# Weights loaded beside their low parts, one explicit order of calls per engine, and a causal mask added in float32r instead of bfloat16

## The chip, the cores and the metric

The kernel runs on one core of a Trainium2 chip. A core has a matrix engine (TensorE, in the profile PE, with its weight loads apart as PEld), a vector engine (VectorE, DVE), an activation engine (ScalarE, ACT), a general engine (GpSimd, POOL) and a queue engine (SyncE, SP) that issues transfers. Each engine works through its own list of instructions in order, and waits on semaphores for the others. The metric is the device time of one execution in microseconds (us), lower is better.

## What is computed

One pre-norm decoder layer on x of 8 batch elements x 256 tokens x 256 features, all in float32:

```python
x = x + attn(layernorm(x))        # 16 heads of 16, rotary positions, causal mask, softmax
x = x + xattn(layernorm(x), ctx)  # 16 heads of 64, 77 context rows, a mask of (8, 256, 77)
x = x + ffn(layernorm(x))         # 256 -> 1024 -> 256, gelu, weights fake-quantised to 8 bits, plus LoRA
...
def fake_quant_weight(w, bits=BITS):
    qmax = 2.0 ** (bits - 1) - 1
    scale = jnp.max(jnp.abs(w)) / qmax
    wq = jnp.clip(jnp.round(w / scale), -qmax - 1, qmax) * scale
```

## The kernel before, in words

**Precision.** Most products are made of three float32r products: a tensor is split into a high part (a copy to float32r by ACT, `split_hi` for weights) and a low part (the tensor less its high part, by DVE, `split_lo` for weights), and `product` on PE adds high x high, high x low and low x high.

**Elements and steps.** The 8 batch elements pass through a pipeline. `step(a, b, n, m)` works at once on the causal attention of element a, on the cross attention and feed-forward part (FFN) of element b = a - 1, on the projections and rotary turn of n = a + 1, and on the first normalisation of m = a + 2. `first()` fills the pipeline, then come `step(0, None, 1, 2)`, `step(1, 0, 2, 3)`, a hardware loop of four equal steps, two steps in which less and less is left to prefetch, and `step(None, 7, None, None)`, which has only the cross attention and FFN of the last element. What stands ahead of `step(1, 0, 2, 3)` is called the start here. Each engine has its own `first` and `step`, and the order of calls in these is the order of its instructions: nothing else schedules.

**The start.** Besides element 0's attention it prepares nine weights. `load_raw` brings a weight into one of two staging halves of `work`; from the third weight on the queue waits for the weight before the last to be split (`w_lo`). Seven of the nine are loaded by POOL's queue, from where POOL also stores the keys and values of the context (`store_keys`, `store_values`) into a scratch tensor in memory. `keys` and `values2` compute these for all elements at once. The two FFN weights are quantised: `largest` (DVE, a row maximum), `quantiser` (POOL, a maximum over partitions), `scale`, three `quantise` parts and `add_lora` (DVE), the LoRA product itself by `lora_up` and `lora_down` on PE.

**Causal attention of one element.** PE's `scores` adds per pair of heads a mask of -2^100 above the diagonal, by a product of an identity with a table, and then the products of queries and keys; DVE's `maxima` takes each row's largest value, `split_max` and `transpose_max` turn it, SP writes it into `q_stack` beside the queries. Then `shifted` (PE) makes the transposed scores less the maximum, `exponentials` (ACT) their exp, `causal` (POOL) zeroes what lies above the diagonal, `weigh` (PE) multiplies by the values, `unnormalised` (ACT) copies, `turn_a` (PE), `attention` (DVE), `turn_back_a`, `output_a` (PE) and `residual_a` (DVE) follow, then `statistics_b` and `norm_b`.

**Cross attention of one element**, in four groups g of heads: `scores2` (PE), `softmax2` (DVE), `exponentials2` (ACT), `sums2` (DVE), `normalise` (POOL), `transpose2` (PE), `probabilities2` (ACT), `weigh2` (PE), `context_hi` (ACT), `context_lo` (DVE), `output2` (PE). The waits that bind most:

```python
pe.wait_ge(c2_lo, 4 * b + g)                      # transpose2(b, g): the group before is split
pe.wait_ge(s_max, H * a + 2 * g - 1)              # scores(a, g): a ring of three banks
dve.wait_ge(rot_ok, 2 * a + w)                    # rotary(a, 1): POOL has read the first half
```

## Time and profile before

| | us |
|---|---|
| median of 3 runs | 733.86 (733.33 to 735.71) |
| the profiled execution | 731.91 |
| its span, first to last instruction | 730.3 |
| PE busy in the span | 580.2 |
| DVE busy | 368.7 |
| ACT busy | 276.5 |
| POOL busy | 189.8 |

The rows further down come from the profiled execution. A row of the timeline gives the start in us from the span's start, the length, the engine, the line of the program, the instruction and its operands (out<-in), and in brackets how long the engine stood idle ahead of it and what ended that. A row by form gives a group's busy time and the mean length in ns. A row of the windows gives each engine's busy time in a stretch and PEclk, the granted TensorE clock as a share of 2.4 GHz.

### The profile page before, as it was taken

Reading aid. Unit: us, or ns where it says so; the run is one execution under the profiler, and the core shown is the slowest. Engines: PE = TensorE matmul, PEld = TensorE weight load, DVE = VectorE, ACT = ScalarE, POOL = GpSimd, SP = SyncE. Lnnn points to the kernel's source line nnn. Section 1 sums busy time; section 2 is a strip of 40 time slices with the busy share of each in tenths; the row PEclk is TensorE's granted clock in tenths of the full one; section 3 lists DMA queues with packets and bytes.
Section 4 is the critical chain, followed back from the end, with each engine's and each line's share of the span. In section 5 each row is a group of like instructions: output and inputs, shape, how many; then the busy total and the mean of one; then the engine's idle time right before and its main releaser. Section 6 shows DMA issues by size and latency. Waiting matters only on the chain.

```text
span 730.3 us, 12418 instructions
## 1 busy us (share of the span) xinstructions
PE 580.2 (79%) x4740; PEld 477.1 (65%) x4740; DVE 368.7 (50%) x711; ACT 276.5 (38%) x419; POOL 189.8 (26%) x295
## 2 busy tenths in 40 slices
PE   3578746498799888987898789878996899688756
PEld 3475323476587657865796579656975687568546
DVE  4455434675347633674357435743575247525521
ACT  2242241233454245333633463336343533363313
POOL 4433223041404122312232223223321301130210
PEclk9789655799799959997999989988998799999968
DMA  6756736020413041203211331123012310200000
GB/s 208 180 185 254 240 116 104 0 87 2 106 37 101 1 99 45 99 1 73 68 67 34 68 73 57 44 55 86 34 54 47 96 31 1 48 9 15 1 0 15
DMA packets 53077, 51.86 MB, mean 71 GB/s; under 512 B 22753, under 2 KB 48769, under 8 KB 53041
## 3 DMA queue, kind: packets, MB, share of 16 engines
q1 hardware_dynamic: 49120, 35.40, 18.9%
q0 software_dynamic: 3920, 15.97, 6.2%
q8 instruction: 24, 0.39, 0.2%
q14 instruction: 13, 0.10, 0.0%
HBM read 33.04 MB, written 18.06 MB: 70 GB/s over the span
## 4 chain that ended last, share of the span: by engine, by line
PE 60%; DVE 16%; issue 8%; ACT 7%; POOL 3%; DMA 1%; POOLq 0%; DVEq 0%; ACTq 0%
PE banks L518 13%; PE banks L519 11%; PE banks L520 11%; PE banks L649 4%; PE banks L744 3%; PE banks L755 3%; DVE mneg L1249 3%; PE banks L662 3%; PE banks L628 3%; DVE c_lo L1208 2%; ACT probs L993 2%; PE banks L622 2%; POOL probs L456 2%; DVE sm L1326 2%; PE banks L699 1%
## 5 line engine op out<-in xcount | busy, mean ns | idle before, releaser
L1249 DVE TENSOR_REDUCE mneg<-banks 128x3 f32<-128x384 f32 x128 | 66.3, 546 | 34.1 <-PE banks L628 34.1
L445 POOL TENSOR_TENSOR work<-work,rc 128x616 f32<-128x616 f32 x32 | 38.9, 1217 | 163.5 <-DVE rc L1328 163.5
L993 ACT ACTIVATE probs<-banks 128x768 f32<-128x768 f32 x64 | 50.1, 811 | 79.1 <-PE banks L649 78.2
L456 POOL TENSOR_SCALAR_AFFINE_SELECT probs<-probs 128x256 f32<-128x256 f32 x128 | 51.2, 430 | 99.5 <-ACT probs L993 99.5
L1208 DVE TENSOR_TENSOR q_lo<-work,q_hi 128x512 fp32r<-128x512 f32 x32 | 22.1, 689 | 73.5 <-ACT q_hi L957 73.5
L518 PE MATMUL banks<-k_hi,q_hi 128*128 128x256 f32 (+1 forms) x160 | 52.7, 329 | 4.3 <-DVE wpj_lo L1182 2.2
L744 PE MATMUL banks<-ident,work 128*77 128x128 f32 x256 | 35.4, 282 | 25.8 <-DVE c_lo L1208 19.7
L957 ACT ACTIVATE work<-banks 77x1024 f32<-77x1024 f32 x32 | 32.4, 1013 | 53.3 <-PE banks L744 53.3
L518 PE MATMUL banks<-wo_hi,c_hi 128*128 128x256 f32 x128 | 42.0, 328 | 12.3 <-DVE c_lo L1208 12.3
L649 PE MATMUL banks<-q_stack,k_stack 50*128 50x128 f32 (+1 forms) x256 | 40.3, 428 | 9.9 <-ACT probs L993 9.9
L744 PEld LDWEIGHTS banks<-ident,work 128*77 128x77 f32 x256 | 28.3, 149 | 29.7 <-POOL work L445 16.2
L519 PE MATMUL banks<-k_lo,q_hi 128*128 128x256 f32 (+1 forms) x160 | 47.1, 294 | 0.0
L520 PE MATMUL banks<-k_hi,q_lo 128*128 128x256 f32 (+1 forms) x160 | 47.0, 294 | 0.0
L649 PEld LDWEIGHTS banks<-q_stack,k_stack 50*128 50x128 f32 x256 | 27.3, 276 | 25.4 <-ACT probs L993 17.8
L1021 ACT ACTIVATE work<-work 128x616 f32<-128x616 f32 x32 | 22.9, 716 | 55.0 <-DVE work L1320 55.0
L518 PE MATMUL banks<-xbT_hi,wfc_hi 128*128 128x256 f32 x128 | 42.4, 331 | 1.5 <-ACT xbT_hi L957 1.5
L662 PE MATMUL banks<-probs,v_aug 128*32 128x256 f32 x256 | 27.1, 505 | 20.7 <-POOL probs L456 20.7
L1208 DVE TENSOR_TENSOR c_lo<-banks,c_hi 128x512 fp32r<-128x512 f32 x32 | 22.0, 688 | 38.6 <-ACT c_hi L957 38.6
L518 PE MATMUL banks<-xbT_hi,wq_hi 128*128 128x256 f32 x128 | 36.7, 287 | 5.0 <-ACT xbT_hi L957 2.9
L519 PE MATMUL banks<-wo_lo,c_hi 128*128 128x256 f32 x128 | 39.6, 309 | 0.0
L520 PE MATMUL banks<-wo_hi,c_lo 128*128 128x256 f32 x128 | 39.6, 309 | 0.0
L519 PE MATMUL banks<-xbT_lo,wfc_hi 128*128 128x256 f32 x128 | 39.0, 305 | 0.0
(184 smaller groups left out, 1684.1 us busy)
## 6 DMA issues: line engine op xcount, KB each, us to landing
rot_dram<-rot_s_hi SPq DMA_DIRECT2D x16, 256.0 KB, 2.1
rot_dram<-rot_s_lo SPq DMA_DIRECT2D x16, 256.0 KB, 2.1
q_stack<-rot_dram SPq DMA_DIRECT2D x32, 128.0 KB, 2.7
k_stack<-rot_dram SPq DMA_DIRECT2D x32, 128.0 KB, 3.2
k_hi<-k_dram SPq DMA_DIRECT2D x16, 154.0 KB, 3.3
k_lo<-k_dram SPq DMA_DIRECT2D x16, 154.0 KB, 3.6
v<-v_dram SPq DMA_DIRECT2D x8, 308.0 KB
x_in<-in_x SPq DMA_DIRECT2D x8, 256.0 KB, 3.0
```

What stands on the lines that cost most here:

```text
L445: pool.tensor_tensor(sc2[g % 2], sc2[g % 2], rc2[:, g % 2].rearrange("p g a -> p g a ()").broadcast_to([P, 4, 2, S2]), ALU.mult).then_inc( ...
L456: last = pool.affine_select(out=diagonal, in_=diagonal, compare_op=ALU.is_ge, fill=0.0, base=0, pattern=[[0, 2], [1, P]], channel_multipli ...
L518: pe.matmul(dst, w[0], x_[0], start=first, stop=False, **kw)
L519: pe.matmul(dst, w[0], x_[1], start=False, stop=False, **kw)
L520: return pe.matmul(dst, w[1], x_[0], start=False, stop=last, **kw)
L649: mm = pe.matmul(halves(bk + p)[:, 1 - k, k * P:T], k_stack[rows, g, k * P:(k + 1) * P], q_stack[rows, g, k * P:T], start=(k == 1), stop=( ...
L662: pe.matmul(dst[32 * j:32 * j + 32, :], v_aug[:, 0, 4 * g + j, :], probs[:, (4 * g + j) % 8, P:3 * P], start=True, stop=False, skip_group_ ...
L744: mm = pe.transpose(bank[0:S2, 5 + c, p * T + q * P:p * T + (q + 1) * P], sc2[g % 2][:, c * QT + q, p, :], ident[:])
L957: act.activation(dst, src, ACT.Copy).then_inc(done, 1)
L993: act.activation(probs[:, n:n + 2, :], bank[:, bk:bk + 2, P:4 * P], ACT.Exp, scale=SCALE).then_inc(p_ok, 1)
L1208: dve.tensor_tensor(dst, src, hi.bitcast(F32), ALU.subtract).then_inc(done, 1)
L1249: dve.tensor_reduce(mneg[:, :, h % 2, h // 2], bank[:, h % 3, 0:3 * P].rearrange("p (c n) -> p c n", n=P), AX_X, ALU.max, negate=True).the ...
```

## The change

It has five parts.

1. Weights in place: each weight is loaded into the memory that later holds its own low part (`raws`), so nine staging areas take the place of two, with a semaphore each. SP issues all loads, most of them at once. The key and value stages lie elsewhere (`k_slots`, `v_stage`), keys are stored by SP, one store per block of 128.
2. `step(0, None, 1, 2)` is gone; its calls stand in `first()`, mixed with those of elements 0 and 1 and the weights. The low parts of the two FFN weights are made by POOL (`split_lo` there) at the end of the start, in place of DVE. `lora_up`, `lora_down` and `add_lora` come in four pieces each.
3. The calls within `step` are in another order on PE, ACT, DVE and POOL. The work of a step is the same.
4. The mask of `scores` is a product of a float32r identity with a float32r table.
5. `rotary(1, 0)` waits for the stores of the last two key blocks, whose stage is `probs`; `norm_b(0, 0)` waits for the stores of the values, whose stage is `work`.

```diff
+        with ExitStack() as before:
+            raws = {name: before.enter_context(nc.sbuf_tensor(name + "_raw", [P, int(np.prod(shape[1:]))], F32))
+                    for name, shape in low_shapes.items()}
+        lows = {name: sb(name + "_lo", shape, F32R) for name, shape in low_shapes.items()}
...
         def load_raw(eng, k, *views):
-            if k >= 2:
-                eng.wait_ge(w_lo, k - 1)
             for dst, src in views:
-                eng.dma_start(dst, src).then_inc(raw_sem[k], 16)
+                eng.dma_start(dst, src).then_inc(w_ld[k], 16)
...
                 for bk in banks:
-                    pe.matmul(bank[:, bk, P:3 * P], ident_bf[:], causal_qk[:].rearrange("p a n -> p (a n)"),
+                    pe.matmul(bank[:, bk, P:3 * P], ident_r[:], causal_r[:].rearrange("p a n -> p (a n)"),
                               start=True, stop=False, skip_group_check=True)
...
@@ gpsimd @@
+            def split_lo(k):
+                pool.wait_ge(w_hi[k], 1)
+                pool.tensor_tensor(split_to[k][1], raw_of[k], split_to[k][0].bitcast(F32),
+                                   ALU.subtract).then_inc(w_lo[k], 1)
...
@@ tensor, the start @@
             def first():
-                transpose_a(0)
-                pe.wait_ge(w_lo, QKV_W + 1)
-                project(0, 0)
-                project(0, 1)
+                transpose_a(0)
+                keys(0)
+                keys(1)
+                project(0, 0)
+                keys(2)
+                keys(3)
+                project(0, 1)
...
@@ scalar, the end of the start @@
+                exponentials(0, 6, 2)
+                unnormalised(0, 0, 2)
+                exponentials(0, 7, 2)
+                unnormalised(0, 1, 2)
+                attention_hi(0)
+                split_hi(PJ_W)
+                split_hi(WQ_W)
+                xaT_part(2)
+                values(1)
+                split_hi(FC_W)
...
@@ tensor, step @@
+                scores(a, 4, rotated)
+                output2(b, 0)
+                weigh2(b, 1)
+                scores(a, 5, rotated)
+                scores2(b, 3)
+                transpose2(b, 2)
+                scores(a, 6, rotated)
+                output2(b, 1)
+                weigh2(b, 2)
...
@@ vector, step @@
+                xbT_part(b, 0)
+                mask_bias(b)
+                rotary(n, 0)
+                queries(b, 0)
+                queries(b, 1)
+                rotary(n, 1)
+                softmax2(b, 0)
+                queries(b, 2)
+                sums2(b, 0)
+                maxima(a, 0)
```

PE in `step(1, 0, 2, 3)`, around the third `transpose2` (line 744 before, 795 after): the end of `scores2` for the fourth group (products of k2 and q2), `scores` of a pair (causal mask, then k_stack), `output2` (wo2). Before:

```order
L518 MATMUL banks<-k2_hi,q2_hi 128x256
L519 MATMUL banks<-k2_lo,q2_hi 128x256
L520 MATMUL banks<-k2_hi,q2_lo 128x256
L622 MATMUL banks<-causal_qk,ident_bf 128x256 x2
L628 MATMUL banks<-k_stack,q_stack 128x256 x2
L628 MATMUL banks<-k_stack,q_stack 128x128 x2
L744 MATMUL banks<-ident,work 77x128 x8
L518 MATMUL banks<-wo2_hi,c2_hi 128x256
```

and after:

```order
L562 MATMUL banks<-k2_hi,q2_hi 128x256
L563 MATMUL banks<-k2_lo,q2_hi 128x256
L564 MATMUL banks<-k2_hi,q2_lo 128x256
L795 MATMUL banks<-ident,work 77x128 x8
L669 MATMUL banks<-causal_r,ident_r 128x256 x2
L675 MATMUL banks<-k_stack,q_stack 128x256 x2
L675 MATMUL banks<-k_stack,q_stack 128x128 x2
L562 MATMUL banks<-wo2_hi,c2_hi 128x256
```

`scores` stood between `scores2` and `transpose2`, and now stands ahead of `scores2`, with the next one behind `transpose2` and ahead of `output2`.

DVE at the end of the start, from the quantising of the second FFN weight (wscale, winv, the three passes over 2048 columns, the LoRA sum) to the attention output of element 0 (rc_a, attn). Before:

```order
L1150 TENSOR_REDUCE wmax<-work 128x1
L1155 TENSOR_SCALAR wscale<-wmax 128x1
L1157 RECIPROCAL winv<-wscale 128x1
L1164 TENSOR_SCALAR work<-work,winv 128x2048
L1166 TENSOR_SCALAR work<-work 128x2048
L1168 TENSOR_SCALAR work<-work,wscale 128x2048
L1174 SCALAR_TENSOR_TENSOR work<-banks,work 128x2048
L1265 RECIPROCAL rc_a<-banks 128x32
L1268 TENSOR_TENSOR attn<-banks,rc_a 128x256 x2
L1208 TENSOR_TENSOR attn_lo<-banks,attn_hi 128x512
L1145 TENSOR_TENSOR wpj_lo<-work,wpj_hi 128x2048
```

and after:

```order
L1234 TENSOR_SCALAR wpj_raw<-wpj_raw,winv 128x2048
L1216 TENSOR_TENSOR wo2_lo<-wo2_raw,wo2_hi 128x2048
L1236 TENSOR_SCALAR wpj_raw<-wpj_raw 128x2048
L1238 TENSOR_SCALAR wpj_raw<-wpj_raw,wscale 128x2048
L1245 SCALAR_TENSOR_TENSOR wpj_raw<-banks,wpj_raw 128x512 x4
L1340 RECIPROCAL rc_a<-banks 128x32
L1343 TENSOR_TENSOR attn<-banks,rc_a 128x256 x2
L1216 TENSOR_TENSOR wo_lo<-wo_raw,wo_hi 128x512
L1281 TENSOR_TENSOR attn_lo<-banks,attn_hi 128x512
```

The maximum of this weight and its scale are no longer at this place: they stand some 30 rows earlier, among the products of the keys and the `maxima`, and wpj_lo has left DVE.

POOL at the same place, from the last zeroing of element 0's probabilities (AFFINE_SELECT) to the rotary turn of step 1 (rot). Before:

```order
L456 AFFINE_SELECT probs<-probs 128x256 x8
L385 ISA
L385 ISA wmax<-wmax 128x1
L441 ISA
L441 TENSOR_TENSOR rs_b<-rs_b,half_a 128x2
L430 TENSOR_TENSOR rot<-probs 128x256
L431 TENSOR_TENSOR rot<-probs 128x256
```

and after:

```order
L483 AFFINE_SELECT probs<-probs 128x256 x4
L468 TENSOR_TENSOR rs_b<-rs_b,half_a 128x2
L449 TENSOR_TENSOR wfc_lo<-wfc_raw,wfc_hi 128x2048
L449 TENSOR_TENSOR wpj_lo<-wpj_raw,wpj_hi 128x2048
L457 TENSOR_TENSOR rot<-probs 128x256
L458 TENSOR_TENSOR rot<-probs 128x256
```

The maximum over partitions (wmax) has moved ahead of the attention, and two splits of 2048 columns stand ahead of the rotary turn.

## Rows read from the trace of the kernel before

**Rows 1.** The page, its head: span of the profiled execution.

```profile
span 730.3 us, 12418 instructions
```

**Rows 2.** Windows: start, six full steps, the step without prefetch.

```profile
core 0: us, PE busy (x) PEld busy (x) DVE busy (x) ACT busy (x) POOL busy (x), PEclk, DMA share, GB/s
0.00:142.80 142.80, 85.70 (x434) 63.77 (x434) 69.53 (x102) 40.91 (x57) 44.72 (x71) 0.74 0.55 164
142.80:594.70 451.90, 391.69 (x3418) 326.09 (x3419) 238.94 (x495) 185.88 (x286) 122.07 (x190) 0.92 0.22 59
594.70:663.90 69.20, 57.52 (x533) 47.09 (x531) 35.35 (x73) 28.86 (x44) 14.47 (x25) 0.98 0.08 19
```

**Rows 3.** Timeline from 88 to 142 us, all engines.

```profile
88.84 0.79 PE L649 MATMUL banks<-q_stack,k_stack 50*128 50x128 f32 x4
...
93.81 0.77 POOL L252 DMA_DIRECT2D work<-in_wQ  x1 [9.68 <-DVE wo_lo L1145]
...
99.09 1.08 PE L662 MATMUL banks<-probs,v_aug 128*32 128x256 f32 x8 [6.05 <-POOL probs L456]
...
106.90 7.19 PE L570 MATMUL banks<-x,v 16*128 16x256 f32 x16
...
124.53 0.38 POOL L385 PARTITION_ALL_REDUCE wmax<-wmax  x1 [6.23 <-issue]
...
131.44 0.35 DVE L1265 RECIPROCAL rc_a<-banks 128x32 f32<-128x32 f32 x1
...
141.29 0.74 DVE L1203 TENSOR_SCALAR work<-x,mv_b,rs_b 128x256 f32<-128x256 f32 x2 [1.01 <-POOL rs_b L441]
```

**Rows 4.** Timeline of PE in one full step, where it waited longest.

```profile
473.99 1.07 PE L744 MATMUL banks<-ident,work 128*77 128x128 f32 x8 [1.34 <-DVE c_lo L1208]
...
485.52 0.35 PE L518 MATMUL banks<-wo_hi,c_hi 128*128 128x256 f32 x1 [1.53 <-DVE c_lo L1208]
...
508.86 0.66 PE L681 MATMUL banks<-ident,attn 128*128 128x128 f32 x4 [1.39 <-DVE attn L1268]
```

**Rows 5.** Windows of the same step: up to the last output2, and the exponentials.

```profile
444.50:487.70 43.20, 37.23 (x337) 30.86 (x336) 27.52 (x51) 14.73 (x21) 11.01 (x11) 0.98 0.14 44
487.70:502.00 14.30, 12.43 (x97) 8.45 (x96) 5.49 (x16) 7.47 (x10) 6.85 (x17) 0.57 0.48 120
```

**Rows 6.** Windows, the first 20 us.

```profile
0.00:20.00 20.00, 7.10 (x40) 6.38 (x40) 10.32 (x16) 5.68 (x5) 9.21 (x19) 1.00 0.67 224
```

**Rows 7.** Groups by form: weight splits on DVE, splits of 512 columns on POOL.

```profile
L1145 DVE TENSOR_TENSOR wq_lo<-work,wq_hi 128x2048 fp32r<-128x2048 f32 x2 | 4.8, 2389 | 1.3 <-ACT wq_hi L935 1.3
L436 POOL TENSOR_TENSOR rot_s_lo<-rot,rot_s_hi 128x512 fp32r<-128x512 f32 x16 | 20.5, 1282 | 21.1 <-ACT rot_s_hi L957 21.1
```

**Rows 8.** Lines 1257 and 417: ns min/median/max, first and last start.

```profile
L1257 DVE CAST mneg_s<-mneg x8: 182/182/2020, 78.9 to 628.8; 128x32 fp32r<-128x32 f32 x8
...
L417 POOL MEMSET k_lo<- x1: 1226/1226/1226, 79.6 to 79.6; 128x1334 f32 x1
```

**Rows 9.** Timeline around one scores, PE and PEld.

```profile
229.61 0.28 PE L520 MATMUL banks<-xbT_hi,wq_lo 128*128 128x256 f32 x1
...
229.73 0.12 PEld L622 LDWEIGHTS banks<-causal_qk,ident_bf 128*128 128x128 bf16 x2
229.73 0.39 PE L622 MATMUL banks<-causal_qk,ident_bf 128*128 128x256 bf16 x2
...
230.05 0.45 PE L628 MATMUL banks<-k_stack,q_stack 48*128 48x256 f32 x4
```

**Rows 10.** Groups by form: weight loads of float32 operands.

```profile
L519 PEld LDWEIGHTS banks<-k_lo,q_hi 128*128 128x128 f32 x160 | 31.7, 198 | 0.0
```

**Rows 11.** Timeline of a full step's first third: rotary, exp and sums.

```profile
449.12 0.69 DVE L1239 TENSOR_TENSOR probs<-banks,cos_t 128x512 f32<-128x512 f32 x1 [1.00 <-POOL rot L431]
...
454.74 1.28 ACT L1021 ACT_TABLE_LOAD   x1
...
457.14 0.56 DVE L1249 TENSOR_REDUCE mneg<-banks 128x3 f32<-128x384 f32 x1 [0.51 <-PE banks L628]
```

More of the change, by code:

```diff
@@ new lines, in first @@
+                lora_up(3)
+                lora_down(0)
+                lora_down(1)
+                shifted(0, 0)
+                shifted(0, 1)
+                shifted(0, 2)
+                shifted(0, 3)
+                weigh(0, 0)
+                shifted(0, 4)
+                shifted(0, 5)
+                weigh(0, 1)
+                shifted(0, 6)
+                lora_down(2)
+                shifted(0, 7)
+                lora_down(3)
+                weigh(0, 2)
+                weigh(0, 3)
@@ L820, in step @@
-                if A and not B:
-                    for pr in range(XM):
-                        keys(pr)
+                transpose_b(b, 0)
+                if N:
+                    project(n, 0)
+                    project(n, 1)
+                queries(b, 0)
+                queries(b, 1)
+                queries(b, 2)
+                scores2(b, 0)
+                queries(b, 3)
                 if A:
                     scores(a, 0, rotated)
-                if B:
-                    scores2(b, 1)
+                scores2(b, 1)
@@ L866, in step @@
+                weigh2(b, 2)
                 if A:
                     scores(a, 7, rotated)
[L868 to L870 removed]
+                transpose2(b, 3)
+                output2(b, 2)
                 if A:
                     transpose_max(a)
[L873 to L883 removed]
@@ L918, in step @@
-                if A and not B:
-                    pe.wait_ge(w_lo, PJ_W + 1)
+                project_down(b, 2)
+                project_down(b, 3)
             elements(first, step)(pe)
@@ L1088, in step @@
[L1088 to L1098 removed]
+                xbT_part(b, 0)
+                queries(b, 0)
+                queries(b, 1)
@@ L1383, in step @@
                 if A:
                     maxima(a, 0)
-                if A and not B:
-                    largest(0, FC_W)
-                if B:
-                    sums2(b, 0)
-                    queries(b, 3)
-                    softmax2(b, 1)
-                if A:
-                    for h in range(1, 4):
-                        maxima(a, h)
-                if B:
-                    sums2(b, 1)
+                queries(b, 3)
+                if A:
+                    maxima(a, 1)
+                    maxima(a, 2)
@@ L1396, in step @@
+                softmax2(b, 1)
+                if A:
+                    maxima(a, 3)
+                sums2(b, 1)
                 if A:
                     maxima(a, 4)
+                context_lo(b, 0)
+                if A:
                     maxima(a, 5)
-                if A and not B:
-                    scale(0, FC_W)
-                if B:
-                    context_lo(b, 0)
-                    softmax2(b, 2)
-                if A:
-                    for h in range(6, 9):
-                        maxima(a, h)
@@ L1407, in step @@
-                if A and not B:
-                    quantise(0, FC_W, 0)
-                if B:
-                    sums2(b, 2)
+                    maxima(a, 6)
+                    maxima(a, 7)
+                softmax2(b, 2)
+                if A:
+                    maxima(a, 8)
+                sums2(b, 2)
+                context_lo(b, 1)
                 if A:
```

765 lines of the change are left out of this document (404 added, 361 removed).

## Prediction

> **What bounds the kernel now.** The profiled execution took 731.91 us for a span of 730.3 [rows 1]; the median of the runs shown is 733.86, 2 us above it. I make the sum against 731.91 and add the 2 us at the end. A measurement of this kernel can tell about 0.3% (2.2 us) from no change.
>
> I first cut the span by the program's stages, with the windows [rows 2]. The start takes 142.8 us, and there no engine is the bound: PE is busy for 85.7 us, much of it at a mean granted clock of 0.74, DVE for 69.5. Six full steps take 451.9 us, 75.3 each, PE busy 87% of them at 0.92. The step without prefetch takes 69.2. So the start is a chain of waits, and the steps are PE plus its waits.
>
> For the start I then read the timeline where PE stands idle [rows 3]. The first `shifted` is at 88.84. POOL sat 9.68 us in a load of a weight, because the queue waited for a split on DVE; the zeroing of the probabilities is behind it on POOL, so PE waited 6.05 us before the first `weigh`. At 106.90 `lora_down` takes 7.19 us in one block. The last `weigh` ends near 120.4. Then POOL's maximum over partitions ends at 124.9, DVE quantises the second FFN weight, and only at 131.44 does the attention output of element 0 begin (rc_a). Element 0's second normalisation is at 141.29. That row is my milestone for the end of the start.
>
> In a full step, 444.5 to 520, PE's ten gaps of 0.3 us and more sum to 9.9 us. Three of the ten stand in [rows 4]: two of the waits for the low part of a group's context, and that for the attention output. The part up to the last `output2` takes 43.2 us at clock 0.98, and the 14.3 us of the exponentials run at 0.57 [rows 5], that is mostly at 1.2 GHz, after the gaps just named.
>
> **The change, part by part.**
>
> *The start up to the first `shifted`.* The weights are issued at once. Ahead of the end of the key weight stand 3.0 MB (x, three 256 KB projections, two rotary tables, the context, 1 MB of keys), which at the 224 GB/s of the first 20 us [rows 6] is 13.3 us, with a landing some 15. ACT's high part (1.9 us) and DVE's low part (2.4 us, [rows 7]) put the first key product at 19, and the first projection, at 12.4 before, at 25. By laying the new lists against each other with the lengths of the old trace I find the keys done at 50, `rotary(1, 0)` held until their stores land at 54, the first `scores` at 61, paced from there by DVE (16 maxima of 0.55 us and 3.7 us of quantising between), the last maximum at 76, and the first `shifted` at 81.5, since two of the four `lora_up` products and two of the four `lora_down` pieces stand ahead of it. Before: 88.84. I take -7; bounds are -14 (PE at full clock throughout, where it had 0.74) and +3 (all 7.19 us of `lora_down` ahead of it, and loads 3 us late).
>
> *From there to the last `weigh`.* 31.6 us before. The 6.05 us wait goes with the loads on POOL's queue; two weight splits of 1.9 us between the exponentials on ACT go; half of `lora_down` (3.6 us) has gone ahead. What stays is a ring of one bank for element 0, 1.7 us for each of eight `shifted`, four `weigh` of 1.6 and 3.6 of `lora_down` partly under ACT: about 20. So -11.5, bounds -8 and -14.
>
> *From the last `weigh` to the attention output.* 120.4 to 131.44, 11 us, of which the copy of the second half, the turn and its start need 3.3. The rest was the maximum on POOL and 6.5 us of DVE work (124.9 to 131.44), now done before. -7.7. From rc_a to the normalisation nothing shrinks: a weight split of 0.7 us is added to DVE while it waits for ACT. In all -26: the milestone at 115.
>
> *POOL's two splits.* Before, DVE made them in 2.3 us each, one of them under waits. On POOL 512 columns take 1.28 us [rows 7], so 2048 take 4.6 to 5.1 us and both 9.7. They begin when ACT has copied the last FFN weight and end about 126.5. Behind them in POOL's list is the rotary turn of step 1, behind that, through `rot_ok`, DVE's `rotary(2, 1)`, and behind that DVE's `softmax2(0)` and PE's `scores`. DVE would be there at 123; it goes on at 128.2. +5.5, with bounds 0 and +9.7 (nothing, or all of it, on the path).
> A row shows what else POOL can do to DVE. A cast of 0.18 us took 2.02 us while POOL cleared the keys [rows 8]. The Trainium skill ("SBUF — State Buffer", section "SBUF: two separate sides") says the two share a port pair as an exclusive lock, for DVE work in a two-port mode or with two SBUF inputs; this trace agrees in that row. By that rule `mask_bias` and the split of the query weight would stand behind POOL's splits, and the stall would be 9.7, the upper bound, not 5.5. I keep 5.5, because what DVE does there is ahead of `rotary(2, 1)`, which waits for POOL anyway.
>
> *The mask.* The pair of bfloat16 products begins at 229.73, the next product at 230.05: 0.32 us, where float32r products of the same 256 columns follow each other every 0.12 (229.61 to 229.73) [rows 9]. The float32 weight load of 0.198 us is hidden at that pace [rows 10]. So the pair should take 0.24: -0.08 for each of 64 `scores`, 5 us in all if all lay on the path, 0.6 per step. Bound on the other side: both loads of a pair lie open, 0.396 us for the 0.12 in which the two bfloat16 loads begin and end, so +0.28, less the 0.08: +0.2 a pair, 12.8 us over 64.
> The Trainium skill ("TensorE: Matmul & The Clock Gate", section "Weight-path perf modes — Fast Weight Load (FWL) and DoubleRow") says the fast load is on for 128 weights of a type other than FP32. By it the change gives the fast load away and the sum would be 12.8 us worse and not 5 better. The trace agrees that the float32 load is the longer one, but not that the pace suffers from it.
>
> *The order in a step, first part* (43.2 us). `scores2` of group 3 now runs while ACT and DVE split the context of group 1, so the wait of 1.34 us goes. The two near 480 and 485 shrink from 3.0 to about 0.5, because `context_lo` stands earlier among the maxima; a new wait of 0.75 comes at the last `scores`. One wait grows: `maxima(a, 0)` now stands behind `sums2(0)`. Laid out: `rotary(n, 1)`, 4.6 us into the step before [rows 11], is now at 7.7; POOL's turn, ACT's copy, the table load of 1.28 and exp follow, and maximum 0 is done 14.7 us in (13.2 before), so the second `scores` begins at 14.85 and not 14.2. Sum of this part with the mask: 40.1 for 43.2, -3.1.
>
> *Second part* (32.3 us). `project_down(0)` fills the wait for the attention output (1.39), `hidden(1)` that for the last zeroing (1.05), while an extra `shifted` runs ahead of the first `weigh`. The exponentials stay paced by ACT (eight of 0.81), so I expect the low clock there again. -1.7; 0 if the waits only move, -5 if the clock stays up: 14.3 us at 0.57 is up to 6 us of loss.
>
> A full step: -4.8, or 70.5 us. Six: -29. The step without prefetch: -3. The last step has none of the maxima, and is a chain through all engines; ACT's exp of group 1 now waits for the copy of group 0. I take 0, bounds -1 and +2.
>
> **The sum.** 731.9 - 26 + 5.5 - 29 - 3 = 679.4, and 2 for the median: **681**.
>
> **Rivals.**
> (A) Only the start gains. The waits in a step move and don't shrink, as the order of calls adds no resource. For it: PE is busy 87% already, and one wait grows. Against: the gaps are waits for work that has slack behind it. 731.9 - 26 + 5.5 + 2 = 713.
> (B) The steps gain more: fewer gaps ahead of the exponentials keep the clock up. Six times another 3 us: 663, to 650 with a start at its lower bound.
> (C) The start gains 10 us only, because the loads, now together, come late for keys and projections, and PE is cold again and again: 697.
> (D) The mask is dearer, with the load exposed: 681 + 5 + 12.8 = 699.
> (E) Slower. Place: the second `scores` of each step, held by maximum 0 behind `sums2(0)`, exp, table load, ACT's copy, POOL's turn and `rotary(n, 1)`, which has moved behind two `queries` splits. What it delays (the ring of three banks) shifts all later maxima and the shift of the scores. The start gives 20.5 net, so the kernel is slower from 3 us lost in each of seven steps; at 4 us it is 731.9 - 20.5 + 28 + 2 = 741. Against it: by the rows this chain is 1.5 us later than before and PE has 0.6 us of it.
>
> **How the numbers follow.** Forecast 0.60 (666 to 696), A 0.11, B 0.13, C 0.07, D 0.04, E 0.05. The range leaves out E, half of A and the far end of B: 657 to 711. Faster by over 0.3% 0.93 (all but E and some of its edge), within 0.3% 0.02, slower 0.05.
>
> **What would show it.** Right: the second normalisation of element 0 at 110 to 121 us; results of full steps 70 to 71 us apart, the first some 5 longer with DVE idle for POOL's rot near 8 us into it; the product behind the mask pair 0.24 us after its start; no long wait at the third `transpose2`. Wrong: steps still 75 us apart (A), a granted clock near 1 in the exponentials (B), DVE or PE waiting for a load before 50 us (C), 0.4 us or more for the mask pair (D), PE waiting over 3 us at the second `scores` (E).

## The result

The changed kernel takes 681.46 us (median of 4 runs, 677.97 to 683.4), the kernel before 734.79 us beside it (4 runs, 733.33 to 735.81). The ratio is 0.9287, with a 95% interval of 0.9249 to 0.9324. The forecast was 681 us in a range of 657 to 711. The profiled execution has a span of 676.3 us and took 677.97, to be held against the sum of 679.4. In the table further down, two executions count as slow, over 1.5% above the fastest of their kernel (679.62 with the bfloat16 mask, 671.78 with that and the splits on DVE): they are in the medians and left out of the ratios.

The windows of the changed kernel, cut at the second normalisation of element 0 and then at each element's result, answer to [rows 2]. The columns are: stretch and length, then for each engine its busy time and instructions, PEclk (TensorE's mean granted clock), DMA share, GB/s.

```profile
core 0: us, PE busy (x) PEld busy (x) DVE busy (x) ACT busy (x) POOL busy (x), PEclk, DMA share, GB/s
0.00:123.50 123.50, 86.31 (x434) 65.89 (x434) 60.51 (x104) 39.47 (x57) 34.17 (x58) 0.78 0.59 190
123.50:198.90 75.40, 65.42 (x572) 56.19 (x573) 50.42 (x87) 31.45 (x48) 30.31 (x33) 0.91 0.24 56
...
198.90:271.10 72.20, 66.47 (x574) 56.41 (x572) 40.41 (x86) 31.20 (x48) 21.04 (x32) 0.91 0.22 62
271.10:339.00 67.90, 62.10 (x572) 52.49 (x570) 40.30 (x85) 31.20 (x48) 20.99 (x32) 0.97 0.26 65
339.00:408.40 69.40, 63.60 (x572) 53.92 (x571) 40.36 (x85) 31.21 (x48) 20.98 (x32) 0.95 0.26 64
408.40:479.20 70.80, 65.00 (x572) 54.87 (x571) 40.38 (x86) 31.21 (x48) 20.99 (x32) 0.93 0.26 62
...
548.10:613.90 65.80, 60.62 (x533) 50.15 (x534) 35.55 (x73) 29.06 (x44) 14.81 (x25) 0.92 0.09 20
```

The start ends at 123.5 instead of 141.29 [rows 3], so it is 17.8 us shorter, not 26. In other profiled executions with this order in the start, it lies between 119.36 (the bfloat16 mask) and 125.23 (the changed kernel again), so this number carries some 2 to 4 us of chance either way. The first step is 75.4 us long, and DVE is busy in it for 50 us, where the full steps behind it have 38 to 40. The five full steps behind it have a mean of 69.8 us (the fifth, 68.9 us, is not among the rows shown and has somewhat less to prefetch). They differ by 4.3 us, and their order by length is that of PEclk: 67.9 us at 0.97, 69.4 and 68.9 at 0.95, 70.8 at 0.93, 72.2 at 0.91.

The timeline of the changed kernel from 61 us on (start, duration, engine, line, operation; in brackets the idle time before it and what ended it) shows the milestones of the start. L669 is the mask pair, L606 `lora_up`, L613 `lora_down`, L1324 a maximum, L696 `shifted`, L712 `weigh`.

```profile
61.94 0.40 PE L669 MATMUL banks<-causal_r,ident_r 128*128 128x256 f32 x2
...
80.23 3.10 PE L606 MATMUL banks<-q_raw,x 16*128 16x512 f32 x4
80.34 1.02 DVE L1324 TENSOR_REDUCE mneg<-banks 128x3 f32<-128x384 f32 x2 [0.25 <-PE banks L675]
...
83.79 3.78 PE L606 MATMUL banks<-q_raw,x 16*128 16x512 f32 x4
...
87.37 3.62 PE L613 MATMUL banks<-x,q_raw 16*128 16x256 f32 x8
...
90.92 0.79 PE L696 MATMUL banks<-q_stack,k_stack 50*128 50x128 f32 x4
...
109.63 0.66 PE L712 MATMUL banks<-probs,v_aug 128*32 128x128 f32 x8
...
113.01 0.36 DVE L1340 RECIPROCAL rc_a<-banks 128x32 f32<-128x32 f32 x1 [4.71 <-PE banks L721]
...
123.49 0.73 DVE L1276 TENSOR_SCALAR work<-x,mv_b,rs_b 128x256 f32<-128x256 f32 x2
```

The first `scores` is on time (61.94, forecast 61). The first `shifted` is at 90.92, 9.4 us late: TensorE works through `lora_up` and two pieces of `lora_down` ahead of it, 10.3 us from 80.23 to 90.56, at a mean PEclk of 0.54, which is 1.2 GHz for most of it. From there on the forecast fits: the last `weigh` ends 19.4 us later (forecast 20) and the attention output begins 2.7 us after that (forecast 3.3).

Behind the start, the same timeline shows what POOL's two splits meet.

```profile
124.13 2.29 DVE L1216 TENSOR_TENSOR wq_lo<-wq_raw,wq_hi 128x2048 fp32r<-128x2048 f32 x1
...
125.21 5.67 POOL L449 TENSOR_TENSOR wfc_lo<-wfc_raw,wfc_hi 128x2048 fp32r<-128x2048 f32 x1 [2.61 <-ACT wfc_hi L1001]
...
126.93 8.56 DVE L1362 TENSOR_SCALAR mask_bf<-mask_u 128x154 bf16<-128x154 uint8 x2
...
130.81 4.58 POOL L449 TENSOR_TENSOR wpj_lo<-wpj_raw,wpj_hi 128x2048 fp32r<-128x2048 f32 x1
...
137.94 0.44 PE L778 MATMUL banks<-mask_bf,ident_bf 128*128 128x154 bf16 x2 [4.42 <-DVE q_lo L1281]
```

DVE's pair for the mask bias takes 8.56 us, where one of its instructions takes 0.234 at the median. The first begins at 126.93 inside POOL's first split and ends at 130.9, as that split does (130.88); the second takes 4.59 us and ends at 135.49, with the end of POOL's second split (135.39). TensorE waits 4.42 us for DVE's split of the queries (q_lo), which stands behind the pair.

In the step from 408.4 on, TensorE's longest waits answer to [rows 4].

```profile
423.10 0.51 PE L669 MATMUL banks<-causal_r,ident_r 128*128 128x256 f32 x2 [1.08 <-DVE mneg L1324]
...
442.31 1.07 PE L795 MATMUL banks<-ident,work 128*77 128x128 f32 x8 [0.64 <-DVE c_lo L1281]
...
447.54 0.36 PE L562 MATMUL banks<-wo_hi,c_hi 128*128 128x256 f32 x1 [1.53 <-DVE c_lo L1281]
```

The 1.34 us at the third `transpose2` and the 1.39 us at the attention output are gone. The 1.53 us at the last `output2` is still there, to the hundredth. The second `scores` waits 1.08 us for maximum 0, 14.7 us into the step.

### The profile page after: what moved, and what is told of

Same layout as the page of the kernel before. It is cut to its first block, busy times and chain, and to the rows that moved or that the text cites. A ratio compares the mean times of both kernels' runs of the same rounds, so it can differ in the third digit from the quotient of the medians.

```text
span 676.3 us, 12427 instructions
## 1 busy us (share of the span) xinstructions
PE 576.2 (85%) x4740; PEld 481.6 (71%) x4740; DVE 370.9 (55%) x715; ACT 276.3 (41%) x419; POOL 192.1 (28%) x284
## 4 chain that ended last, share of the span: by engine, by line
PE 72%; DVE 9%; ACT 7%; issue 5%; POOL 4%; DMA 1%; SPq 0%; ACTq 0%; POOLq 0%; DVEq 0%
PE banks L562 15%; PE banks L563 13%; PE banks L564 13%; PE banks L806 5%; PE banks L795 5%; PE banks L709 4%; PE banks L696 3%; PE banks L675 2%; PE banks L669 2%; PE banks L712 2%; PE banks L748 2%; DVE c_lo L1281 1%; ACT work L1021 1%; ACT probs L1056 1%; DVE work L1276 1%
## 5 line engine op out<-in xcount | busy, mean ns | idle before, releaser
L1324 DVE TENSOR_REDUCE mneg<-banks 128x3 f32<-128x384 f32 x128 | 66.3, 548 | 11.2 <-PE banks L675 11.0
L562 PE MATMUL banks<-wo_hi,c_hi 128*128 128x256 f32 x128 | 40.3, 314 | 12.3 <-DVE c_lo L1281 12.3
L696 PE MATMUL banks<-q_stack,k_stack 50*128 50x128 f32 (+1 forms) x256 | 38.0, 393 | 11.5 <-ACT probs L1056 11.5
L696 PEld LDWEIGHTS banks<-q_stack,k_stack 50*128 50x128 f32 x256 | 24.3, 240 | 26.7 <-ACT probs L1056 17.0
L795 PE MATMUL banks<-ident,work 128*77 128x128 f32 x256 | 34.5, 278 | 7.3 <-DVE c_lo L1281 4.6
L564 PE MATMUL banks<-xbT_hi,wfc_lo 128*128 128x256 f32 x128 | 38.9, 304 | 0.0
L562 PEld LDWEIGHTS banks<-k_hi,q_hi 128*128 128x128 f32 x160 | 32.6, 204 | 8.4 <-issue 5.3
L806 PE MATMUL banks<-work,v 77*32 77x256 f32 x512 | 34.3, 385 | 4.6 <-ACT work L1021 4.6
L669 PE MATMUL banks<-causal_r,ident_r 128*128 128x256 f32 x128 | 30.1, 316 | 9.0 <-DVE mneg L1324 8.8
L562 PEld LDWEIGHTS banks<-wo_hi,c_hi 128*128 128x128 f32 x128 | 25.3, 198 | 17.0 <-ACT c_hi L1021 15.9
```

Source lines behind the costliest of these rows:

```text
L562: pe.matmul(dst, w[0], x_[0], start=first, stop=False, **kw)
L564: return pe.matmul(dst, w[1], x_[0], start=False, stop=last, **kw)
L669: pe.matmul(bank[:, bk, P:3 * P], ident_r[:], causal_r[:].rearrange("p a n -> p (a n)"), start=True, stop=False, skip_group_check=True)
L696: mm = pe.matmul(halves(bk + p)[:, 1 - k, k * P:T], k_stack[rows, g, k * P:(k + 1) * P], q_stack[rows, g, k * P:T], start=(k == 1), stop=( ...
L795: mm = pe.transpose(bank[0:S2, 5 + c, p * T + q * P:p * T + (q + 1) * P], sc2[g % 2][:, c * QT + q, p, :], ident[:])
L806: mm = pe.matmul(halves(5)[32 * j:32 * j + 32, c, :], v2[:, col:col + 32], p2T[:, 2 * c + j // 2, :], start=True, stop=True, skip_group_ch ...
```

## The experiments

All ratios are to the kernel before, measured beside each kernel on its chip, where its medians were 733.09 to 734.79 us. A ratio is estimated from all executions of both kernels and need not be the quotient of two medians.

| kernel | median us (lowest to highest) | ratio | 95% interval |
|---|---|---|---|
| changed kernel | 681.46 (677.97 to 683.4) | 0.9287 | 0.9249 to 0.9324 |
| the same again | 680.28 (677.7 to 683.39) | 0.9268 | 0.9225 to 0.9311 |
| old order in the steps | 724.64 (721.88 to 726.97) | 0.9862 | 0.9818 to 0.9906 |
| new order in the steps alone | 687.48 (685.03 to 694.29) | 0.9383 | 0.9334 to 0.9432 |
| bfloat16 mask | 675.19 (667.85 to 679.62) | 0.9159 | 0.9104 to 0.9213 |
| float32r mask alone | 734.36 (733.21 to 739.35) | 1.0003 | 0.9974 to 1.0033 |
| mask bias early | 676.68 (673.09 to 678.32) | 0.9209 | 0.9171 to 0.9247 |
| splits on DVE | 669.60 (665.27 to 672.44) | 0.9122 | 0.9084 to 0.9160 |
| low-rank products later | 679.85 (676.55 to 684.94) | 0.9267 | 0.9224 to 0.9311 |
| old second part of a step | 697.90 (697.33 to 700.19) | 0.9508 | 0.9473 to 0.9543 |
| splits on DVE, bfloat16 mask | 663.78 (661.79 to 671.78) | 0.9059 | 0.9006 to 0.9112 |
| splits on DVE, products later | 669.18 (668.12 to 670.28) | 0.9121 | 0.9083 to 0.9160 |
| all three | 668.29 (664.12 to 669.95) | 0.9089 | 0.9047 to 0.9131 |

**Old order in the steps.** The changed kernel's `first()`, buffers and mask, with `step` on every engine as before:

```diff
-                transpose_b(b, 0)
-                if N:
-                    project(n, 0)
-                    project(n, 1)
+                if N:
+                    project(n, 0)
+                transpose_b(b, 0)
+                if N:
+                    project(n, 1)
...
```

> The changed kernel with its start, its buffers and its float32r causal mask, but with the order inside a step written back on all engines as it was before. Theory of the prediction, with the sizes read since from the changed kernel's trace: the start gives some 19 us (the first element's result came at 198.92 instead of 218.20), the order some 33, and the two don't lean on each other. So about 715 us, range 711 to 719, and full steps of about 75 us. Rival, that the step's gain comes from the weights in place or the mask rather than from the order: full steps stay near 70 us and the time is near 685.

724.64 us, 10 below the kernel before and 10 above what I expected. The normalisation of element 0 is at 122.0, as early as with the new order, but the first step takes 86.5 us. The timeline of this kernel shows why.

```profile
135.34 0.69 DVE L1379 TENSOR_TENSOR probs<-banks,cos_t 128x512 f32<-128x512 f32 x1 [8.63 <-POOL rot L462]
...
139.28 0.44 PE L787 MATMUL banks<-mask_bf,ident_bf 128*128 128x154 bf16 x2 [8.00 <-DVE q_lo L1346]
```

In the old order `rotary(2, 1)` stands ahead of all splits of the queries on DVE. It waits for POOL's turn, which stands behind both weight splits, and TensorE waits 8.00 us in the end. So the new start is worth 19.3 us up to the normalisation, and with the old order 9.6 us of that are given back in the next step (86.5 us, where the kernel before has 76.9 from 141.3 to 218.2). The later full steps keep a mean of 75.1 us.

**New order in the steps alone.** The kernel before with its own start and bfloat16 mask; `step(0, None, 1, 2)` keeps the old order:

```diff
-                step(0, None, 1, 2)
+                step0(0, None, 1, 2)
                 step(1, 0, 2, 3)
```

> The kernel before with its own start and its bfloat16 mask, and the new order inside a step from the second step on. Theory: the order alone takes full steps from 75 to 70 us, seven steps give some 33 us, so about 701 us, range 697 to 706. Rival, that the order needs the new start or the new mask: over 710 us.

687.48 us: 46.5 us of gain from the order alone, where I expected 33. The window of its fourth full step, from result to result:

```profile
416.10:485.70 69.60, 63.62 (x573) 53.18 (x572) 40.61 (x86) 31.17 (x48) 20.96 (x32) 0.95 0.26 63
```

Its steps have the lengths of the changed kernel's at the same granted clock, to 0.2 us: 68.0 to 68.1 at 0.97 (67.4 for the fifth, which has less to prefetch), 69.6 at 0.95. Four of its five full steps are at 0.97; of the changed kernel's five, one was.

**Old second part of a step.** The changed kernel, with TensorE, ACT, DVE and POOL in the old order behind the maxima's transposes:

```diff
-                project_down(b, 0)
                 if A:
                     turn_back_a(a)
                 hidden(b, 3)
...
-                project_down(b, 1)
                 if M:
                     transpose_a(m)
-                project_down(b, 2)
-                project_down(b, 3)
+                for g in range(4):
+                    project_down(b, g)
```

> The changed kernel with the second part of a step (from behind the maxima's transposes on) written back as before on all engines, and the new order in the first part. The prediction gave 1.7 us of a full step to the second part and 3.1 to the first, so 6 x 1.7 = 10: 691.5. The trace of the changed kernel has the step's shortening at 5.4 us; read from it, the first part gives 2.2 to 3 and the second 2.4 to 3: 696 to 701, which I take. Rival, all of it from one part: 681.5 or 715.

697.90 us, so 17 us over the two measurements of the changed kernel, 2.4 for each of seven steps. All its full steps ran at a clock of 0.95; this is one of them, and under it the step of the kernel before at that clock.

```profile
347.50:419.30 71.80, 63.38 (x572) 53.78 (x571) 40.64 (x84) 31.38 (x48) 20.62 (x32) 0.95 0.22 61
```

```profile
370.60:444.80 74.20, 63.36 (x573) 52.95 (x572) 40.30 (x84) 31.23 (x48) 20.58 (x32) 0.95 0.24 59
```

At equal clock, then: 74.2 before, 71.8 with the new first part, 69.4 with both. Each part is worth 2.4 us. TensorE's busy time is the same in all three (63.4 to 63.6), so it is waits that went: TensorE's gaps of 0.3 us and more sum to 10.7 us in the step of the kernel before and to 5.2 in the changed kernel's from 339.0 to 408.4. The first of the three has the bfloat16 mask and the others the float32r one; the new order with the bfloat16 mask took 69.6 at this clock (above), so the mask does not carry the difference.

**The changed kernel again.**

> The changed kernel once more, unaltered, beside the three kernels below on one chip, so that the float32r mask can be judged against the spread between executions. Theory A, that the low-clock stretches of TensorE fall differently from one execution to the next and move the time by several us: a median anywhere from 676 to 684, and full steps that lie on the same line of length by lost clock (67.9 us where the clock lost 1.7 us, 69.4 at 3.4, 70.8 at 5.1, 72.1 at 6.8), at other places than in the first profile. Theory B, that the stretches belong to the program: 681.5 within 1 us and the same long steps as before.

680.28 us. Windows of its first and fourth full step:

```profile
205.10:272.90 67.80, 62.02 (x573) 52.63 (x572) 40.10 (x84) 31.18 (x48) 21.07 (x32) 0.97 0.26 66
...
411.80:481.00 69.20, 64.47 (x572) 54.26 (x571) 40.53 (x85) 31.29 (x48) 20.96 (x32) 0.93 0.24 64
```

The first full step, the longest of the first profile (72.2 at 0.91), is now the shortest. Theory A holds for the places of the low stretches. The median hardly moved, though, with single executions from 677.7 to 683.39, and the step at 0.93 was 69.2 us long and not 70.8, so a low stretch costs more or less by what it falls on.

**The mask.** One line each way, in the changed kernel and in the kernel before:

```diff
-                    pe.matmul(bank[:, bk, P:3 * P], ident_r[:], causal_r[:].rearrange("p a n -> p (a n)"),
+                    pe.matmul(bank[:, bk, P:3 * P], ident_bf[:], causal_qk[:].rearrange("p a n -> p (a n)"),
```

> The changed kernel with the causal mask added by bfloat16 products again, nothing else altered. The prediction had float32r 0.08 us cheaper a pair, so 5 us should be lost here: 686.5. The changed kernel's trace has the pair at 0.33 us where nothing was waited for and 0.43 behind a wait, against 0.32 for both before, which makes bfloat16 the same or cheaper by 0 to 0.1 us a pair over 64 pairs: 675 to 681.5, which I now take. The rule that the weight load of float32r is slower, priced at 0.2 us a pair, gives 668.7.

> The kernel before with nothing altered but the causal mask, added by float32r products. By the trace of the changed kernel 0 to +6 us: 735 to 741. By the prediction's term of -0.08 us a pair: 730. By the rule of the slower weight load, +0.2 us a pair: 747.

675.19 and 734.36 us: going back to bfloat16 gains some 6 us in the new order; float32r costs 0.3 us, which is nothing that can be measured, in the old one. The price of a pair, from its start to that of the next product, depends on what stands ahead of it. TensorE in the changed kernel, behind a `product` chain and behind transposes (L795):

```profile
419.34 0.40 PE L669 MATMUL banks<-causal_r,ident_r 128*128 128x256 f32 x2
419.67 0.45 PE L675 MATMUL banks<-k_stack,q_stack 48*128 48x256 f32 x4
...
423.91 1.10 PE L795 MATMUL banks<-ident,work 128*77 128x128 f32 x8
424.76 0.48 PE L669 MATMUL banks<-causal_r,ident_r 128*128 128x256 f32 x2
425.17 0.45 PE L675 MATMUL banks<-k_stack,q_stack 48*128 48x256 f32 x4
```

And with bfloat16 products, behind the same transposes:

```profile
421.35 1.09 PE L795 MATMUL banks<-ident,work 128*77 128x128 f32 x8
422.28 0.38 PE L669 MATMUL banks<-causal_qk,ident_bf 128*128 128x256 bf16 x2
422.60 0.45 PE L675 MATMUL banks<-k_stack,q_stack 48*128 48x256 f32 x4
```

The float32r pair takes 0.33 us up to the next product when a `product` chain with weights of 128 columns stands ahead of it, 0.40 to 0.44 behind transposes, behind `weigh2` and behind a wait. The bfloat16 pair takes 0.32 behind all of them. The lines' weight loads have a median of 189 and 98 ns:

```profile
L669 PEld LDWEIGHTS banks<-causal_r,ident_r x128: 186/189/333, 61.7 to 578.5; 128*128 128x128 f32 x128
```

```profile
L669 PEld LDWEIGHTS banks<-causal_qk,ident_bf x128: 95/98/116, 61.7 to 572.6; 128*128 128x128 bf16 x128
```

At full clock 45 of 62 pairs of the changed kernel took 0.39 us or more, and 17 of 64 with the old order. The means are 0.396 and 0.352 us against 0.318 for bfloat16, which over 64 pairs is 5.0 and 2.2 us of TensorE's time. Step and mask are thus not independent: the new order puts most mask pairs behind short instructions, where the longer load lies open.

How much of the 5.0 us reaches the end can be bounded by comparing at equal clock. The steps at a clock of 0.97 are 67.9 and 67.8 us long with float32r, 67.9 and 68.1 with bfloat16; at 0.95, 69.4 against 69.2. Whole executions can be compared in the same way, since the mean granted clock of each was measured too. At 0.903 and 0.904 the changed kernel took 677.97 and 677.7 us, and at 0.906 the kernel with the bfloat16 mask took 676.49. But the mean clock was 0.896 over the ten executions of the changed kernel and 0.911 over the five with bfloat16 that its ratio counts. So the 6 us are for the most part a difference in clock, and 1.2 us or less are left for the mask here. Whether the mask makes it, or chance, no run here shows.

**Mask bias early, and splits on DVE.** In the first, one pair on DVE is moved to the end of the start. In the second, POOL's two splits become DVE's, in gaps of the start, and ACT's copies (`split_hi`) are moved ahead of them:

```diff
                 attention(0)
                 split_lo(WO_W)
+                mask_bias(0)
```

```diff
-                split_lo(FC_W)
-                split_lo(PJ_W)
...
                 add_lora(1, PJ_W, 1)
+                split_lo(FC_W)
...
                 attention_lo(0)
+                split_lo(PJ_W)
```

> The changed kernel with one DVE pair moved: the mask bias of element 0 (two instructions that take 0.23 us each elsewhere and took 8.56 us together beside POOL's two splits) is made at the end of the start, ahead of the splits. Theory A, that only this pair is held by POOL's splits: TensorE's wait of 4.4 us at the second score block of step 1 goes, part of it comes back at the second rotary, which waits for POOL's rotation until 137: 3 to 4.4 us faster than the changed kernel, 677 to 678.5. Theory B, that POOL's splits hold whatever DVE does there: no gain, 681.5. Theory C, the prediction's own: the stall comes from POOL's late rotation and so the place of the pair is of no account: 681.5, with the wait now in front of the second rotary's products.

> The changed kernel with the low parts of both feed-forward weights made by DVE in gaps of the start (2.3 to 2.4 us each by its other splits of that size, one in the gap of 8.7 us at 96 to 105, one in the gap of 3.0 us at 117 to 120) in place of POOL's two splits at 125 to 135; ScalarE's two splits are moved to its own gaps ahead of them. Theory: both the held mask bias and the late rotation go, and step 1 becomes 5 to 7 us shorter than the 74.7 us from the last start product to its result: 674 to 677 us. Rival, that the gaps on DVE are no gaps for 2.4 us and norm_b of element 0 comes later: gain under 3 us.

676.68 and 669.60 us. The measure of the stall is the way from the normalisation of element 0 to the first maximum of `softmax2`: 17.9 us in the changed kernel (123.49 to 141.43), 14.7 with the mask bias early (120.26 to 134.94), 12.1 with the splits on DVE (122.78 to 134.86). So the stall is 5.9 us, and 3.3 of it were the mask bias. The other 2.6 fit the late rotation, which is the wait that the timeline of the kernel with the mask bias early has left:

```profile
128.14 0.69 DVE L1281 TENSOR_TENSOR q_lo<-banks,q_hi 128x512 fp32r<-128x512 f32 x1 [2.70 <-ACT q_hi L1021]
...
133.73 0.69 DVE L1314 TENSOR_TENSOR probs<-banks,cos_t 128x512 f32<-128x512 f32 x1 [3.48 <-POOL rot L458]
```

At 128.14 DVE works in the middle of POOL's splits (121.99 to 132.23 here) at its usual 0.69 us, so this kind, with one of its two inputs (`banks`) in PSUM, the matrix engine's output memory, is not held. Then it waits 3.48 us for POOL's turn. Theories A and C of the expectation are both true in part, and B is false. With the splits on DVE, the mask bias takes no more than 0.504 us an instruction. The 11 us gained there are more than the 5.9 of the stall, and the rest goes with the clock: its mean over six executions was 0.912, against 0.896 for the changed kernel. At nearly the same clock, 0.905 and 0.904, the two took 672.44 and 677.7 us, 5.3 apart. Why the clock was higher, no run here shows.

**Low-rank products later**, TensorE's order in the start alone:

```diff
-                lora_up(0)
-                lora_up(1)
                 transpose_max(0)
-                lora_up(2)
-                lora_up(3)
-                lora_down(0)
-                lora_down(1)
+                lora_up(0)
+                lora_up(1)
                 shifted(0, 0)
+                lora_up(2)
                 shifted(0, 1)
+                lora_up(3)
                 shifted(0, 2)
+                lora_down(0)
...
```

> The changed kernel with TensorE's order altered in the start alone: the transposes of the maxima go ahead of all four low-rank products up, two of these cover the transfer of the shifts, and the other two and the first two products down stand between the shifted score blocks, where TensorE waits 0.9 us each for ScalarE. Theory, that the 10.3 us of these fp32 products in front of the first shifted block are what the prediction's start missed: the first shifted block at 86 to 87 instead of 90.9, about 0.65 us of it given back in each of four gaps: 2 to 3 us faster, 678.5 to 679.5. Rival, that the shifts land only at 90 or that DVE's scaling of the second weight, put off by this, sets the start's end: no gain.

679.85 us, 1.6 and 0.4 us below the two measurements of the changed kernel: no gain that can be told. The timeline of this kernel shows where it went.

```profile
84.69 0.79 PE L696 MATMUL banks<-q_stack,k_stack 50*128 50x128 f32 x4 [0.55 <-DMA q_stack<-mnegT]
85.42 2.07 PE L606 MATMUL banks<-q_raw,x 16*128 16x512 f32 x2
87.42 0.80 PE L696 MATMUL banks<-q_stack,k_stack 50*128 50x128 f32 x4
```

The first `shifted` comes 6.2 us earlier than in the first profile of the changed kernel (and 3 to 8 us earlier than in all profiled executions with its order there, 87.5 to 92.6), so the products were what held it. It now waits 0.55 us for the shifts' transfer. But at half the clock (PEclk 0.50 from 84 to 90) one call of `lora_up`, two products, takes 2.07 us where the gap was 0.9, and a `shifted` with such a call ahead of it follows the last by 2.73 us and not 1.70. The last of the eight begins at 103.62, against 104.77, so 1.2 us are left of the 6.2.

**Combinations**, the three edits above laid together:

> The kernel whose feed-forward splits are made by DVE (669.6 us), with bfloat16 products for the causal mask. If the mask's number format costs nothing and the 6 us between the two masks in the changed kernel were clock: 669.6 within 2. If float32r costs 0.1 us a pair: 663.

> The kernel whose feed-forward splits are made by DVE, with the low-rank products put between the shifted blocks as well. The two parts lie in different stretches and should add: 1.6 us less than 669.6, so 668, range 665 to 670.

> All three together: splits on DVE, low-rank products between the shifted blocks, bfloat16 mask. If the mask costs nothing 668, if it costs 0.1 us a pair 661.5. Expected to be the fastest of the study or equal to it.

663.78, 669.18 and 668.29 us. On top of the splits, the bfloat16 mask gives 5.8 us, the moved products 0.4. With the splits on DVE and the products later, the bfloat16 mask gives 0.9. With the changed kernel's 6 that makes three comparisons in the new order, all of one sign, 0.9 to 6 us; the intervals of each pair overlap except for the first. The granted clock moved along with them: its mean was higher with the bfloat16 mask in the first two (0.911 against 0.896, 0.919 against 0.912) and lower in the third (0.910 against 0.913). In executions of one mean clock the mask gives 0.3 us in the second (665.27 and 664.95 at 0.922) and 2.4 in the third (668.12 and 665.77 at 0.914). So the float32r mask costs some 0.3 to 2.4 us in the new order, estimated from single executions, and the rest of the differences goes with the clock. The fastest version is the changed kernel with its feed-forward splits on DVE and the bfloat16 mask, 663.8 us; all three edits together can't be told from it.

## Why the prediction was right, and where it wasn't

*The total* was right: 679.4 summed against 677.97 in the profiled execution and 682.23 in that of the repeat. That the direction and the parts that gain were right is the mechanism; that the sum came within 2 us is luck, because errors of opposite sign met: the start gave 8 us less than predicted, and the steps without the stall became 41 us shorter where I had 32 (7.4 us in the first, 27.4 in the five full ones behind it, 3.4 and 2.7 in the last two), and 1.2 us went behind the last result.

*The start*, predicted -26, measured -17.8, with the piece up to the first `shifted` at +2 and not at -7. The step that failed is "paced from there by DVE ..., the last maximum at 76, and the first `shifted` at 81.5". Two sizes in it were off, each by about half of the 9.4 us. The last maxima came at 80.34, as TensorE was the pace there: `values2(3)` ran from 69.4 to 74.4 at a PEclk of 0.53, and DVE waited 3.42 us for the `scores` behind it. And the 10.3 us of `lora_up` and `lora_down` were only in part covered by the shifts' transfer: with the products moved, the first `shifted` began 4.1 us after the maxima's transposes (80.59 to 84.69), and in the changed kernel 7.7 us after them (83.26 to 90.92). All four `lora_up` calls stand ahead of it in the program, where the prediction counted two. The other pieces were -12.2 (predicted -11.5) and -8.3 (predicted -7.7), and 0.6 was added behind them.

*POOL's two splits*, predicted +5.5 with bounds 0 and 9.7, measured +5.9. The size was right, the reason half wrong, and so the size is in part luck. I wrote that what DVE does there "is ahead of `rotary(2, 1)`, which waits for POOL anyway". But `queries(0, 0)` and `queries(0, 1)` stand between the two, and TensorE waits for those. The row on the cast, 2.02 us for 0.18 [rows 8], had shown that POOL's work can hold DVE's, and here each instruction of the pair stood still until the split then running on POOL was done. The Trainium skill ("SBUF — State Buffer", section "SBUF: two separate sides") calls the port pair that the two share an exclusive lock, for DVE work in a two-port mode, or with two inputs in SBUF against a POOL instruction that reads SBUF; the one that starts first has it for its whole length. The rows agree on the three kinds of work at hand: the mask bias held, readers of PSUM not held, and POOL's first split 1.09 us longer than its second where it began 1.21 us before DVE's split of the query weight ended. The stall of 9.7 that I had drawn from that rule did not come with the new order, since TensorE had work until 133.5. A loss of that size, 9.6 us, came with the old order, but by the wait for POOL's turn and not by held DVE work: there the pair ran at 136.55, behind both splits.

*The mask*, predicted -0.08 us a pair, measured +0.08. The step that failed is "So the pair should take 0.24". It took the pace of a chain of products for that of a pair; the float32r load of 189 ns costs nothing to speak of behind products of the `product` chain (0.33 us a pair) and shows behind shorter instructions and waits (0.40 to 0.44). The rule that I weighed against it (the Trainium skill, "TensorE: Matmul & The Clock Gate", section "Weight-path perf modes — Fast Weight Load (FWL) and DoubleRow") has the right sign: the load takes twice as long (189 and 98 ns). The price of 0.2 us a pair, 12.8 in all, that I had worked out with it was too high: 5.0 us of TensorE's time, of which 0.3 to 2.4 reach the end at equal clock.

*The order, first part*, predicted -3.1, measured -2.4 at equal clock. The wait of 1.34 went; the other two, 3.0 us, fell to 2.2 (0.64 and 1.53) and not to 0.5, and the mask's 0.6 was no gain. The second `scores` at 14.7 us into the step was forecast at 14.85.

*The order, second part*, predicted -1.7, measured -2.4 at equal clock. The waits for the attention output (1.39) and for the last zeroing (1.05) went, as forecast.

*The low clock*, predicted to stay as it was. It stayed in kind and shrank in extent, which is a piece of rival B: the changed kernel's steps had 0.91 to 0.97 and those before 0.89 to 0.95. In the stretch of the exponentials, 14.3 us from 2.2 us behind the start of the last `output2`, four full steps of the changed kernel had 0.62, 0.88, 0.76 and 0.64, where [rows 5] has 0.57. Its steps are 1.4 to 1.5 us longer for each 0.02 of mean clock, those before 0.3 to 1.7. With the clock the gain of the order alone rises from 4.6 us at 0.95 (74.2 to 69.6) to 7.1 us a step (75.3 to 68.2), and in the changed kernel from 4.8 to 5.5. That the shorter waits raised the clock is likely, and not shown apart from chance.

*The rivals.* A (only the start gains) is the reverse of what was found: start alone -9.4, order alone -46.5. C (a start that gains 10) holds for the start under the old order, though by POOL's splits and not by late loads. D (a dearer mask) has the sign right and the size wrong: 0.3 to 2.4 us at equal clock, not 18. E did not come: the second `scores` waits 1.08 us.

## What to carry over

A gain at one place is worth what the next queue lets through: 19 us of an earlier start became 10 because the first instruction behind it waited on an engine that had been given the weight splits, and two edits on one engine's list have to be costed together. Before handing elementwise work to POOL, look at what DVE does from SBUF (the on-chip memory that the engines share) to SBUF meanwhile, and at who waits behind it. When a product is swapped for one with a longer weight load, look at what stands ahead of it at every place, since the load is hidden or open by that, and a reordering changes it. Where the clock wanders, compare two versions by executions of the same mean clock.

## What the hardware showed that I had not expected

The low-clock stretches don't belong to a place in the program. Windows of the kernel with the splits on DVE, in two of its full steps, at the same distance from the result before. The columns are the window, its length, PE busy (x instructions), PEclk, DMA share and GB/s:

```profile
370.40:375.40 5.00, 3.07 (x29) 1.00 0.71 138
375.40:380.40 5.00, 5.00 (x48) 0.66 1.09 177
380.40:385.40 5.00, 5.00 (x62) 1.00 0.53 128
...
438.40:443.40 5.00, 3.94 (x26) 0.74 0.67 148
443.40:448.40 5.00, 4.18 (x36) 0.60 0.75 197
448.40:453.40 5.00, 5.00 (x36) 0.50 0.02 5
```

In the five microseconds ahead of these rows TensorE was busy for 3.46 and 3.47 us, and its two longest waits near there were the same in both steps, 0.64 us and 1.53 us for the low parts of the context. In one step the clock is low in a part of one window, in the other it is at 0.74 or less through three, and that step is 4.2 us longer (72.2 against 68.0). With five such draws to a run, a difference of a few us between two executions says nothing of two versions of this kernel: the 39 executions of the kernel before beside these experiments lie between 728.74 and 738.75 us, wider than the 0.3% that the prediction gave a measurement. Comparing executions of the same mean clock takes most of this out. What decides the place of the fall, no run here shows.
